# Layered field interactions: a table of matmul kinds for even, odd and last chunks, fewer low parts on VectorE, other ring depths, and sums stored by fours

## The chip, the cores and the metric

The kernel runs on one core of one Trainium2 chip. The metric is the device time in microseconds (us), as a median over runs. Five engines share the work: TensorE (PE, its weight loads are shown as PEld), VectorE (DVE), ScalarE (ACT), GpSimd (POOL) and SyncE (SP), which here only issues transfers.

## The reference

The input `x0` has 512 examples of 39 fields of 16 numbers. Three layers follow each other, each with 128 outputs:

```
xk = x0
for layer in 0, 1, 2:
    z = relu(einsum('bhd,bkd,hks->bsd', x0, xk, W[layer]) + b[layer])
    if layer < 2:
        xk = z[:, :64]           # goes into the next layer
        direct.append(z[:, 64:]) # is only summed
    else:
        direct.append(z)
logit = sum(concatenate(direct, axis=1), axis=-1)   # over the 16 numbers
```

All of it is in 32-bit floating point. Per layer this is a table of products of pairs of fields, contracted with a weight matrix.

## The kernel before

**Tiles.** The 512 x 16 columns are cut into 16 chunks (`CHUNKS`) of 512 columns (32 examples). For each chunk and layer, VectorE multiplies fields into product tiles of 128 rows x 512 columns, and TensorE contracts them into one accumulator `z`. Two tiles make a couple. Layer 0 has 4 couples (780 distinct pairs; the fourth couple is a rest of 12 rows, kept in 76 rows), layers 1 and 2 have 10 each.

**Kinds.** A couple is done in one of three ways, set by a letter in the tables `KINDS`, `KINDS_FIRST` (chunk 0) and `KINDS_SECOND` (layer 0 of chunk 1):
- E (exact): the product stays 32-bit, and TensorE multiplies it in full precision. Nobody else touches it.
- S: ScalarE rounds the product to a high part `hi` (L656), GpSimd subtracts to get the low part `lo` (L515), and TensorE makes three fast passes for each tile: hi by w_hi, hi by w_lo, lo by w_hi.
- D: as S, but VectorE makes the low part itself (`split_lo`, L440) from a product buffer `d_raw` of which there is one.

The last tile of layers 1 and 2 has no hi by w_lo pass, and the rest couple of layer 0 is one pass in all (its low rows are written into the rows above the high ones, 12 x 512, on GpSimd). The tables of before are "SDES", "ESDSESSDSS", "SSDSSESDES" for every chunk but the first.

**Order.** `segments()` gives the order of couples: layer 1 of chunk c; couples `KEPT` to 9 of layer 2 of chunk c-1 (the tail); layer 0 of chunk c+1; couples 0 to `KEPT`-1 of layer 2 of chunk c. VectorE, ScalarE and GpSimd work in about this order, each ahead of TensorE. The work between two layers of a chunk gives the results time: layer 1 of chunk c must be contracted, and its first 64 outputs copied by ScalarE into `maps2` (L675), before VectorE can begin layer 2 of c.

**Lags.** `schedules()` writes out TensorE's order. The lo passes of a couple come `LO_LAGS[layer]` couples behind its hi passes, and at the end of layer 1 all that are pending follow. `D_LAG` is the number of products between a D product on VectorE and its low part.

**Rings.** Buffers are used in rings: E products, S products (`raw`; freed by GpSimd's low part), high parts and low parts (both freed by the lo passes). `spread` holds field pairs, 7 slots of 1 MB.

**ScalarE's order.** `finish_last(c-1)` (layer 2 of the chunk before, into `final`) stands behind the high parts of couples 0 and 1 of layer 2 of c (`FINISH_AT`). TensorE waits for it before it begins layer 2 of c. `COPY_AT` says where the copy of chunk c+1's fields stands in layer 1, `MAPS1_AT` and `MAPS2_AT` where the outputs of layers 0 and 1 are taken over.

**Weights.** The weights of layers 1 and 2 are split once, in chunks 0 and 1, for those tiles that some table has as S or D (`SPLIT_TILES`): ScalarE makes w_hi (L665), GpSimd w_lo (L531), in pieces (`RUNS`).

**Sums.** VectorE reduces `direct` and `final` over the 16 numbers (L447, L453) into `sums`, [128, 2, 512]. SyncE stores two pieces of 480 columns and at the very end two of 32.

Of the kernel before, what the change touches and what calls it, by code (L numbers as in the profile page):

```python
# [6 lines left out]
BATCH = 512  # L7
OUT = 128
HALF = OUT // 2
COLS = 512  # L10
EXAMPLES = COLS // DIM
CHUNKS = BATCH * DIM // COLS
# [5 lines left out]
BLOCK = 32  # L18
ROWS_REST = 2 * BLOCK + REST
TILES = (FIELDS + 1) // 2  # L20
assert (TILES0 - 1) * 128 + REST == PAIRS
LAYER_TILES = (TILES0, TILES, TILES)

# [2 lines left out]


E, S, D = "E", "S", "D"
KINDS = ("SDES", "ESDSESSDSS", "SSDSSESDES")
KINDS_FIRST = ("EEEE", "ESEEEEEEEE", "EESEEESEES")  # L30

EARLY = 2
KINDS_SECOND = E * EARLY + KINDS[0][EARLY:]
COUPLES = tuple(len(k) for k in KINDS)


def kinds(layer, c):

    if (layer, c) == (0, 1):
        return KINDS_SECOND  # L40
    return KINDS_FIRST[layer] if c == 0 else KINDS[layer]


def split_of(layer, c, couples=None):
# [2 lines left out]

def tiles_of(layer, wanted):

    return [t for t in range(LAYER_TILES[layer]) if any(kinds(layer, c)[t // 2] in wanted for c in (0, 1, 2))]  # L50


SPLIT_TILES = [tiles_of(n, S + D) for n in range(3)]
assert SPLIT_TILES[0][:-1] == list(range(len(SPLIT_TILES[0]) - 1)) and SPLIT_TILES[0][-1] == TILES0 - 1
assert KINDS[0][-1] != E and KINDS_FIRST[0] == E * COUPLES[0]
assert all(KINDS[n][-1] != E for n in (1, 2))

LO_LAGS = (2, 1, 1)
D_LAG = 3

EXACT_RING = 4
RAW_RING = 6
HI_RING = 5
LO_RING = 4
QUADS = TILES // 4
SPREAD_RING = 7
W0_CUTS = (0, 2, TILES0)
W0_PARTS = 2

WEIGHT_CUTS = (0, 4, 8, 12, 16, TILES)  # L70
WEIGHTS_AHEAD = 1
WARM = 3

SUM_LAST_AT = 6
SUM_DIRECT_AT = 6
COPY_AT = 2
FINISH_AT = 2
MAPS1_AT = 5
MAPS2_AT = 3

KEPT = 7
LAST = CHUNKS - 1
assert SUM_DIRECT_AT <= SUM_LAST_AT <= KEPT and MAPS1_AT <= KEPT and FINISH_AT <= MAPS1_AT
FIELD_CUTS = (0, 3, 5, 1 + TILES0)

# [122 lines left out]
def cin_kernel(nc, x_fields, x_spread, w0, w1, w2, b, out):  # L210
# [7 lines left out]
    with ctx:  # L218
        def sb(name, shape, dt=fp32):
            return ctx.enter_context(nc.sbuf_tensor(name, shape, dt))  # L220
# [4 lines left out]
        def sem(name):  # L225
            return ctx.enter_context(nc.semaphore(name))
# [13 lines left out]
        lo = sb("lo", [128, LO_RING, 2, COLS], fp32r)  # L240
        direct = sb("direct", [128, 2, COLS])
        final = sb("final", [128, COLS])
        sums = sb("sums", [128, 2, BATCH])

        w0_staged = raw[:, :, :, :].rearrange("p r t c -> p (r t c)")[:, 0:2 * TILES0 * OUT].rearrange(
            "p (t h s) -> p t h s", h=2, s=OUT)
# [29 lines left out]
        z2_evacuated = sem("z2_evacuated")  # L276
        direct_summed = sem("direct_summed")
        last_summed = sem("last_summed")
        stored = sem("stored")

        def wait_multiplied(engine, layer, c, k):

# [30 lines left out]
        def low_part(layer, c, k):  # L313
# [2 lines left out]
                return hi[low_rows(layer, k), PLACE["SD"][layer, c, k] % HI_RING, 0:1, :]  # L316
            return lo[:, USED[layer, c, k] % LO_RING, :, :]

        def z_of(layer, c):
            return z[{(0, 0): 2, (2, LAST): 0}.get((layer, c), layer)]  # L320

# [6 lines left out]
        @block.sync  # L328
        def _(sp):
            def load_fields(c, p):  # L330
                a, e = FIELD_CUTS[p:p + 2]
                if c == 1:

                    if p == 1:
                        return
                    e = 1 if p == 0 else e
                sp.dma_start(fields[:, a:e, :], x_fields[c, :, a:e, :]).then_inc(fields_loaded[p], 16)  # L337

            def load_early(p):
                a, e = FIELD_CUTS[p:p + 2]  # L340
                sp.dma_start(early[:, a:e, :], x_fields[1, :, a:e, :]).then_inc(early_loaded[p], 16)

            def load_spread(c, q):
                slot, count = quad(c, q)
                if count > 1:
                    before, part = divmod(c * QUADS + q - SPREAD_RING, QUADS)
                    wait_multiplied(sp, 2, before, 2 * part + 1)
                elif slot in (3, 4):
                    wait_multiplied(sp, 0, 1, EARLY - 1)
                sp.dma_start(spread[:, slot, :, :], x_spread[c, :, 4 * q:4 * q + 4, :]).then_inc(  # L350
                    spread_loaded[slot], 16)

            def load_weights(n, p):
                a, e = WEIGHT_CUTS[p:p + 2]
                sp.dma_start(w_exact[n][:, a:e, :], (None, w1, w2)[n][:, a:e, :]).then_inc(w_loaded[n][p], 16)

            load_fields(0, 0)
            sp.dma_start(w0_staged[:, W0_CUTS[1]:, :, :], w0[:, W0_CUTS[1]:, :, :]).then_inc(w0_loaded[1], 16)  # L358
            load_fields(0, 1)
            load_fields(0, 2)  # L360
            load_early(0)
            load_early(1)
            for q in range(QUADS):
                load_weights(1, q)
                load_spread(0, q)
            load_fields(1, 0)
            load_fields(1, 2)
            for p in range(QUADS):
                load_weights(2, p)
            for c in range(LAST):  # L370
                for q in range(2):
                    load_spread(c + 1, q)
                if c + 2 < CHUNKS:
                    wait_multiplied(sp, 0, c + 1, COUPLES[0] - 1)
                    for p in range(3):
                        load_fields(c + 2, p)
                for q in range(2, QUADS):
                    load_spread(c + 1, q)

            done = LAST * EXAMPLES  # L380
            sp.wait_ge(direct_summed, LAST)
            sp.dma_start(out[0:OUT, 0:done], sums[:, 0, 0:done]).then_inc(stored, 16)
            sp.wait_ge(last_summed, LAST)
            sp.dma_start(out[OUT:2 * OUT, 0:done], sums[:, 1, 0:done]).then_inc(stored, 16)
            sp.wait_ge(direct_summed, CHUNKS)
            sp.dma_start(out[0:OUT, done:BATCH], sums[:, 0, done:BATCH]).then_inc(stored, 16)
            sp.wait_ge(last_summed, CHUNKS)
            sp.dma_start(out[OUT:2 * OUT, done:BATCH], sums[:, 1, done:BATCH]).then_inc(stored, 16)
            sp.wait_ge(stored, 64)

        @block.vector
        def _(dve):
# [51 lines left out]
            def sum_direct(c):  # L444
                dve.wait_ge(z0_evacuated, 3 * c + 3)
                dve.wait_ge(z1_evacuated, 3 * c + 3)
                nc.vector.tensor_reduce(sums[:, 0, c * EXAMPLES:(c + 1) * EXAMPLES],  # L447
                                        direct[:, c % 2, :].rearrange("p (b d) -> p b d", d=DIM),
                                        AX.X, ALU.add).then_inc(direct_summed, 1)

            def sum_last(c):
                dve.wait_ge(z2_evacuated, c + 1)
                nc.vector.tensor_reduce(sums[:, 1, c * EXAMPLES:(c + 1) * EXAMPLES],  # L453
                                        final[:, :].rearrange("p (b d) -> p b d", d=DIM),
                                        AX.X, ALU.add).then_inc(last_summed, 1)

            def weights_last_split_lo(n):

                last = len(SPLIT_TILES[n]) - 1
                dve.wait_ge(weights_hi[n], len(RUNS[n]))  # L460
                nc.vector.tensor_tensor(w_hi[n][HALF:128, last, :], w_exact[n][HALF:128, TILES - 1, :],
                                        w_hi[n][HALF:128, last, :].bitcast(fp32),
# [313 lines left out]
```

## Time and profile before

| | before |
|---|---|
| median of 3 runs | 562.28 us (562.15 to 562.33) |
| the profiled execution's own time | 562.33 us |
| its span in the profile | 560.5 us |
| PE busy | 551.9 us, 98% |
| DVE busy | 535.9 us, 96% |
| POOL busy | 499.5 us, 89% |
| ACT busy | 379.4 us, 68% |
| granted TensorE clock, mean | 0.999 |

Busy times count each instruction from its start to its end, and instructions of one engine overlap at their edges: a split pass is listed with 0.39 to 0.40 us, but the next one begins about 0.23 us later. So what an instruction costs is read from the distance between starts. The own time stands 1.8 us above the span.

### The profile page before, as it was taken

To read this page: it belongs to the slowest core of one execution; us is meant where nothing else is said; L and a number is where in the kernel's file an instruction comes from. 1 tells how busy PE (TensorE), PEld (TensorE's weight loads), DVE (VectorE), ACT (ScalarE), POOL (GpSimd) and SP (SyncE) were. 2 spreads that over 40 slices of the span, in tenths; PEclk is the share of its full clock that TensorE was granted. 3 is DMA by queue.
4 is the path that set the end of the run, shared out by engine and by line. 5 is a ranking of instruction groups with operands and counts; after the bars stand their busy time and mean duration, and the time that the engine had idled before them with its cause. 6 is when DMAs were issued, how large, how long until landed. Compare 5 with 4: busy or idle time off the path is not lost.

```text
span 560.5 us, 6190 instructions
## 1 busy us (share of the span) xinstructions
PE 551.9 (98%) x2008; PEld 374.9 (67%) x2008; DVE 535.9 (96%) x496; ACT 379.4 (68%) x427; POOL 499.5 (89%) x228
## 2 busy tenths in 40 slices
PE   7999999999999999999999999999999999999997
PEld 2435667667677677777767677677777767677665
DVE  4679999999999999999999999999999999999985
ACT  0436577776858767676776858777676876858662
POOL 0438899899999989999899999989999899999986
PEclk9999999999999999999999999999999999999999
DMA  8997391844828266391845828276391845826200
GB/s 326 418 408 317 132 370 34 325 191 181 344 87 331 108 254 271 146 361 30 331 183 183 342 95 333 98 262 263 150 363 29 333 177 192 333 99 215 81 1 20
DMA packets 21056, 122.17 MB, mean 218 GB/s; under 512 B 2720, under 2 KB 2976, under 8 KB 10784
## 3 DMA queue, kind: packets, MB, share of 16 engines
q1 hardware_dynamic: 20736, 121.51, 56.0%
q8 instruction: 16, 0.26, 0.2%
q10 hardware_dynamic: 288, 0.26, 0.2%
q14 instruction: 16, 0.13, 0.1%
HBM read 121.24 MB, written 0.52 MB: 217 GB/s over the span
## 4 chain that ended last, share of the span: by engine, by line
PE 82%; DVE 10%; issue 3%; ACT 2%; DMA 1%; POOL 1%; SPq 0%; DVEq 0%; POOLq 0%; ACTq 0%
PE z L611 82%; DVE raw L426 4%; DVE exact L426 3%; DVE d_raw L426 2%; DMA fields<-x_fields 1%; DVE lo L440 1%; POOL lo L515 1%; ACT hi L656 1%; ACT maps L675 0%; ACT final L696 0%; ACT L675 0%; DVE sums L453 0%; DVE sums L447 0%; SPq L358 0%; SPq L337 0%
## 5 line engine op out<-in xcount | busy, mean ns | idle before, releaser
L515 POOL TENSOR_TENSOR lo<-raw,hi 128x1024 fp32r<-128x1024 f32 x198 | 469.1, 2410 | 12.1 <-ACT hi L656 11.6
L656 ACT ACTIVATE hi<-raw 128x1024 fp32r<-128x1024 f32 (+1 forms) x213 | 219.1, 1029 | 125.1 <-DVE raw L426 112.0
L611 PE MATMUL z<-hi,w_hi 128*128 128x512 f32 (+1 forms) x559 | 220.8, 399 | 0.9 <-ACT hi L656 0.4
L426 DVE TENSOR_TENSOR raw<-spread,maps 128x1024 f32<-128x1024 f32 x184 | 219.0, 1210 | 2.1 <-ACT maps L675 2.1
L611 PE MATMUL z<-hi,w_lo 128*128 128x512 f32 x513 | 202.5, 395 | 0.0
L611 PE MATMUL z<-lo,w_hi 128*128 128x512 f32 x544 | 196.7, 451 | 0.2 <-POOL lo L515 0.2
L611 PE MATMUL z<-exact,w_exact 128*128 128x512 f32 (+1 forms) x386 | 180.4, 594 | 2.8 <-DVE exact L426 2.0
L611 PEld LDWEIGHTS z<-lo,w_hi 128*128 128x128 f32 x544 | 101.2, 188 | 56.2 <-issue 31.5
L611 PEld LDWEIGHTS z<-hi,w_hi 128*128 128x128 f32 (+1 forms) x559 | 104.8, 188 | 31.4 <-ACT final L696 3.7
L611 PEld LDWEIGHTS z<-exact,w_exact 128*128 128x128 f32 (+1 forms) x386 | 72.1, 189 | 68.0 <-issue 53.7
L611 PEld LDWEIGHTS z<-hi,w_lo 128*128 128x128 f32 x513 | 96.2, 188 | 22.9 <-issue 0.5
L426 DVE TENSOR_TENSOR exact<-spread,maps 128x1024 f32<-128x1024 f32 x76 | 91.4, 1212 | 8.2 <-ACT maps L675 5.7
L656 ACT ACTIVATE hi<-d_raw 128x1024 fp32r<-128x1024 f32 x74 | 75.8, 1025 | 21.5 <-DVE d_raw L426 18.7
L440 DVE TENSOR_TENSOR lo<-d_raw,hi 128x1024 fp32r<-128x1024 f32 x74 | 89.9, 1215 | 0.0
L426 DVE TENSOR_TENSOR d_raw<-spread,maps 128x1024 f32<-128x1024 f32 x60 | 73.3, 1221 | 0.5
L675 ACT ACTIVATE maps<-z,bias 64x512 f32<-64x512 f32 x64 | 41.5, 648 | 3.4 <-PE z L611 2.2
L515 POOL TENSOR_TENSOR hi<-raw,hi 12x512 fp32r<-12x512 f32 x15 | 19.2, 1279 | 18.5 <-ACT hi L656 18.4
L531 POOL TENSOR_TENSOR w_lo<-w_exact,w_hi 128x512 fp32r<-128x512 f32 (+3 forms) x10 | 9.9, 1001 | 22.7 <-ACT w_hi L665 22.7
L426 DVE TENSOR_TENSOR raw<-fields,copies 76x512 f32<-76x512 f32 (+1 forms) x29 | 27.1, 934 | 0.0
L679 ACT ACTIVATE direct<-z,bias 64x512 f32<-64x512 f32 x32 | 21.9, 685 | 0.8
L426 DVE TENSOR_TENSOR exact<-fields,copies 128x1024 f32<-128x1024 f32 x15 | 18.2, 1212 | 0.0
L426 DVE TENSOR_TENSOR d_raw<-fields,copies 128x1024 f32<-128x1024 f32 x14 | 17.1, 1222 | 0.0
(21 smaller groups left out, 69.6 us busy)
## 6 DMA issues: line engine op xcount, KB each, us to landing
spread<-x_spread SPq DMA_DIRECT2D x80, 1024.0 KB, 8.1
fields<-x_fields SPq DMA_DIRECT2D x31, 768.0 KB, 6.8
fields<-x_fields SPq DMA_DIRECT2D x15, 512.0 KB, 5.6
w_exact<-w SPq DMA_DIRECT2D x10, 256.0 KB, 14.7
spread<-x_fields SPq DMA_DIRECT2D x1, 768.0 KB, 10.1
raw<-w SPq DMA_DIRECT2D x1, 640.0 KB, 6.7
spread<-x_fields SPq DMA_DIRECT2D x1, 512.0 KB, 10.7
out<-sums SPq DMA_DIRECT2D x2, 240.0 KB, 4.2
```

What stands on the lines that cost most here:

```text
L426: nc.vector.tensor_tensor(products, by_field, by[0:rows, :].unsqueeze(1).to_broadcast([rows, tiles, COLS]), ALU.mult).then_inc(ready, 1)
L440: nc.vector.tensor_tensor(low_part(layer, c, k), d_raw[low_rows(layer, k), 0:tiles_in(layer, k), :], hi[low_rows(layer, k), place % HI_RIN ...
L515: nc.gpsimd.tensor_tensor(low_part(layer, c, k), raw[low_rows(layer, k), PLACE[S][layer, c, k] % RAW_RING, 0:tiles_in(layer, k), :], hi[lo ...
L531: nc.gpsimd.tensor_tensor(w_lo[n][:, m:m + e - a, :], w_exact[n][:, a:e, :], w_hi[n][:, m:m + e - a, :].bitcast(fp32), ALU.subtract).then_ ...
L611: mm = nc.tensor.matmul(z_of(layer, c)[:, :], w[0:rows, :], part[0:rows, :], start=(step == FIRST_STEP[layer, c] and p == 0), stop=(step = ...
L656: nc.scalar.activation(hi[0:rows, count % HI_RING, 0:tiles, :], products, ACT.Copy).then_inc(hi_ready, 1)
L675: nc.scalar.activation(maps[half * HALF:(half + 1) * HALF, :], z_of(n, c)[0:HALF, :], ACT.Relu, bias=bias[0:HALF, n:n + 1]).then_inc(evacu ...
L679: nc.scalar.activation(direct[n * HALF:(n + 1) * HALF, c % 2, :], z_of(n, c)[HALF:OUT, :], ACT.Relu, bias=bias[HALF:OUT, n:n + 1]).then_in ...
```

## The change

Four things change together.

1. Tables. Even chunks (from 2): "DSES", "SDESSDSSES", "SSDSSESESS". Odd chunks: "DSES", "SDSSESSDES", "SDSSESDESS". Last chunk (15): "SDES", "SDSSSSSDES", "DSESESDSSD". First chunk: "EEEE", "EEEEEEESEE", "EESEESESES". So an even chunk has 4 D instead of 5, an odd one 5, the last 6.
2. Order and depth: `LO_LAGS` (2, 1, 1) to (0, 2, 1); `D_LAG` 3 to 2; rings of E products 4 to 3, S products 6 to 4, high parts 5 to 6, low parts 4 to 5; `KEPT` 7 to 6; `COPY_AT` 2 to 7; `WEIGHTS_AHEAD` 1 to 2.
3. More weight tiles are split, since more couples are S or D in some chunk: 18 tiles of layer 1 (16 before) and 20 of layer 2 (16 before).
4. `sums` is a ring of 8 chunks, and every four chunks are stored at once: SyncE issues two stores of 128 columns (64 KB each) in its loop at c = 5, 9 and 13, and two at the end. VectorE waits for a store before it writes over its place (`wait_stored`).

```diff
+LAST = CHUNKS - 1
-KINDS = ("SDES", "ESDSESSDSS", "SSDSSESDES")
-KINDS_FIRST = ("EEEE", "ESEEEEEEEE", "EESEEESEES")
+KINDS = ("DSES", "SDESSDSSES", "SSDSSESESS")
+
+KINDS_ODD = ("DSES", "SDSSESSDES", "SDSSESDESS")
+KINDS_LAST = ("SDES", "SDSSSSSDES", "DSESESDSSD")
+KINDS_FIRST = ("EEEE", "EEEEEEESEE", "EESEESESES")
...
-KINDS_SECOND = E * EARLY + KINDS[0][EARLY:]
+KINDS_SECOND = E * EARLY + KINDS_ODD[0][EARLY:]
...
-    return KINDS_FIRST[layer] if c == 0 else KINDS[layer]
+    return (KINDS_FIRST if c == 0 else KINDS_LAST if c == LAST else KINDS_ODD if c % 2 else KINDS)[layer]
...
-LO_LAGS = (2, 1, 1)
-D_LAG = 3
-
-EXACT_RING = 4
-RAW_RING = 6
-HI_RING = 5
-LO_RING = 4
+LO_LAGS = (0, 2, 1)
+D_LAG = 2
+
+EXACT_RING = 3
+RAW_RING = 4
+HI_RING = 6
+LO_RING = 5
...
-WEIGHTS_AHEAD = 1
+WEIGHTS_AHEAD = 2
...
-COPY_AT = 2
+COPY_AT = 7
...
-KEPT = 7
-LAST = CHUNKS - 1
+STORED = 4
+
+
+KEPT = 6
...
-        sums = sb("sums", [128, 2, BATCH])
+        sums = sb("sums", [128, 2, 2 * STORED * EXAMPLES])
...
+        def columns(c):
+
+            a = c % (2 * STORED) * EXAMPLES
+            return slice(a, a + EXAMPLES)
+
+        def wait_stored(engine, half, c):
+
+            if c >= 2 * STORED and c % STORED == 0:
+                engine.wait_ge(stored[half], 16 * (c // STORED - 1))
...
+            def store(half, part):
+
+                a = part * STORED * EXAMPLES
+                sp.wait_ge((direct_summed, last_summed)[half], (part + 1) * STORED)
+                sp.dma_start(out[half * OUT:(half + 1) * OUT, a:a + STORED * EXAMPLES],
+                             sums[:, half, columns(part * STORED).start:columns(part * STORED).start
+                                  + STORED * EXAMPLES]).then_inc(stored[half], 16)
...
-            done = LAST * EXAMPLES
-            sp.wait_ge(direct_summed, LAST)
-            sp.dma_start(out[0:OUT, 0:done], sums[:, 0, 0:done]).then_inc(stored, 16)
...
+                if c > STORED and c % STORED == 1:
+                    for half in range(2):
+                        store(half, c // STORED - 1)
+            for half in range(2):
+                store(half, CHUNKS // STORED - 1)
+            for half in range(2):
+                sp.wait_ge(stored[half], 16 * CHUNKS // STORED)
```

## Rows read from the trace of the kernel before

**Rows 1.** The page's head: span, then busy time and instructions of each engine

```profile
span 560.5 us, 6190 instructions
PE 551.9 (98%) x2008; PEld 374.9 (67%) x2008; DVE 535.9 (96%) x496; ACT 379.4 (68%) x427; POOL 499.5 (89%) x228
```

**Rows 2.** Busy time by stretch, the steady part: PE, PEld, DVE, ACT, POOL, clock, DMA

```profile
75.00:500.00 425.00, 424.61 (x1607) 299.95 (x1607) 424.56 (x393) 308.35 (x342) 406.93 (x178) 1.00 0.56 218
```

**Rows 3.** Chain that ended last: start, length, engine, work

```profile
75.62 427.99 PE z L611 x1620
...
545.87 11.40 PE z L611 x41
```

**Rows 4.** Timeline of DVE: start, length, work [idle before it]

```profile
79.35 0.67 DVE L447 TENSOR_REDUCE sums<-direct 128x32 f32<-128x512 f32 x1
...
304.77 0.68 DVE L426 TENSOR_TENSOR raw<-fields,copies 76x512 f32<-76x512 f32 x1
305.37 1.21 DVE L440 TENSOR_TENSOR lo<-d_raw,hi 128x1024 fp32r<-128x1024 f32 x1
306.50 2.34 DVE L426 TENSOR_TENSOR raw<-spread,maps 128x1024 f32<-128x1024 f32 x2
...
515.91 0.67 DVE L447 TENSOR_REDUCE sums<-direct 128x32 f32<-128x512 f32 x1
516.50 0.67 DVE L453 TENSOR_REDUCE sums<-final 128x32 f32<-128x512 f32 x1
...
538.65 2.35 DVE L426 TENSOR_TENSOR raw<-spread,maps 128x1024 f32<-128x1024 f32 x2 [2.11 <-ACT maps L675]
```

**Rows 5.** Timeline of PE, matmuls

```profile
39.89 3.67 PE L611 MATMUL z<-exact,w_exact 128*128 128x512 f32 x8 [0.80 <-issue]
...
298.46 0.63 PE L611 MATMUL z<-lo,w_hi 128*128 128x512 f32 x2
...
299.86 0.63 PE L611 MATMUL z<-lo,w_hi 128*128 128x512 f32 x2
...
302.90 1.88 PE L611 MATMUL z<-exact,w_exact 128*128 128x512 f32 x4
...
305.07 0.40 PE L611 MATMUL z<-hi,w_hi 128*128 128x512 f32 x1
...
540.61 0.96 PE L611 MATMUL z<-hi,w_hi 128*128 128x512 f32 x2
...
545.87 0.73 PE L611 MATMUL z<-lo,w_hi 128*128 128x512 f32 x2 [0.23 <-POOL lo L515]
```

**Rows 6.** Waits between 75 and 500 us: engine, waited for, total, times, longest

```profile
POOL hi L515 <- ACT hi L656: 14.3, 12, 1.2
PEld z L611 <- POOL lo L515: 5.2, 25, 0.2
POOL lo L515 <- ACT hi L656: 3.5, 22, 0.2
PEld z L611 <- ACT final L696: 3.5, 13, 0.8
```

**Rows 7.** Timeline of POOL

```profile
308.88 26.03 POOL L515 TENSOR_TENSOR lo<-raw,hi 128x1024 fp32r<-128x1024 f32 x11
...
341.02 1.28 POOL L515 TENSOR_TENSOR hi<-raw,hi 12x512 fp32r<-12x512 f32 x1 [1.19 <-ACT hi L656]
...
541.04 11.86 POOL L515 TENSOR_TENSOR lo<-raw,hi 128x1024 fp32r<-128x1024 f32 x5 [2.08 <-ACT hi L656]
553.53 2.35 POOL L515 TENSOR_TENSOR lo<-raw,hi 128x1024 fp32r<-128x1024 f32 x1 [0.64 <-ACT hi L656]
```

**Rows 8.** Groups by line: the splitting of the weights, count, busy, mean ns

```profile
L531 POOL TENSOR_TENSOR w_lo<-w_exact,w_hi 128x512 fp32r<-128x512 f32 (+3 forms) x10 | 9.9, 1001 | 22.7 <-ACT w_hi L665 22.7
```

**Rows 9.** Transfers: count, KB each, median us to landing

```profile
out<-sums SPq DMA_DIRECT2D x2, 240.0 KB, 4.2
out<-sums SPq DMA_DIRECT2D x2, 16.0 KB, 1.6
```

More of the change, by code:

```diff
@@ L48, in tiles_of @@
 def tiles_of(layer, wanted):
-    return [t for t in range(LAYER_TILES[layer]) if any(kinds(layer, c)[t // 2] in wanted for c in (0, 1, 2))]
+    return [t for t in range(LAYER_TILES[layer]) if any(kinds(layer, c)[t // 2] in wanted for c in (0, 1, 2, 3, LAST))]
 SPLIT_TILES = [tiles_of(n, S + D) for n in range(3)]
 assert SPLIT_TILES[0][:-1] == list(range(len(SPLIT_TILES[0]) - 1)) and SPLIT_TILES[0][-1] == TILES0 - 1
-assert KINDS[0][-1] != E and KINDS_FIRST[0] == E * COUPLES[0]
-assert all(KINDS[n][-1] != E for n in (1, 2))
-LO_LAGS = (2, 1, 1)
-D_LAG = 3
-EXACT_RING = 4
-RAW_RING = 6
-HI_RING = 5
-LO_RING = 4
+assert all(k[0][-1] != E for k in (KINDS, KINDS_ODD, KINDS_LAST)) and KINDS_FIRST[0] == E * COUPLES[0]
+assert all(k[n][-1] != E for k in (KINDS, KINDS_ODD, KINDS_LAST) for n in (1, 2))
+LO_LAGS = (0, 2, 1)
[4 more added lines that the diff above has]
+LO_RING = 5
 QUADS = TILES // 4
@@ L278, in cin_kernel @@
         last_summed = sem("last_summed")
-        stored = sem("stored")
+        stored = [sem("stored_direct"), sem("stored_last")]
         def wait_multiplied(engine, layer, c, k):
@@ L378, in _ @@
                     load_spread(c + 1, q)
-            done = LAST * EXAMPLES
-            sp.wait_ge(direct_summed, LAST)
-            sp.dma_start(out[0:OUT, 0:done], sums[:, 0, 0:done]).then_inc(stored, 16)
[L383 to L389, printed above, removed]
+                if c > STORED and c % STORED == 1:
[5 more added lines that the diff above has]
+                sp.wait_ge(stored[half], 16 * CHUNKS // STORED)
         @block.vector
@@ L446, in sum_direct @@
                 dve.wait_ge(z1_evacuated, 3 * c + 3)
-                nc.vector.tensor_reduce(sums[:, 0, c * EXAMPLES:(c + 1) * EXAMPLES],
+                wait_stored(dve, 0, c)
+                nc.vector.tensor_reduce(sums[:, 0, columns(c)],
                                         direct[:, c % 2, :].rearrange("p (b d) -> p b d", d=DIM),
@@ L452, in sum_last @@
                 dve.wait_ge(z2_evacuated, c + 1)
-                nc.vector.tensor_reduce(sums[:, 1, c * EXAMPLES:(c + 1) * EXAMPLES],
+                wait_stored(dve, 1, c)
+                nc.vector.tensor_reduce(sums[:, 1, columns(c)],
                                         final[:, :].rearrange("p (b d) -> p b d", d=DIM),
```

## Prediction

> **What bounds the kernel now.** I read the page's head first: PE is busy 98% of the span, DVE 96%, POOL 89% [rows 1]. Between 75 and 500 us both PE and DVE are busy 99.9% of the time and POOL 96%, at full clock [rows 2]. Busy shares can't tell the two apart, since a pass's listed time hides a bubble of up to 0.16 us behind it. So I count starts.
>
> The period of a chunk is the distance of the sums over `direct`: from 79.35 to 515.91 us is 13 chunks, 33.58 us each [rows 4].
>
> PE's own work: two starts that are one split couple apart are 298.46 and 299.86 us, 1.40 us for six passes, 0.2335 us each. From 302.90 to 305.07 us stand one E couple and two lo passes: 2.17 - 0.47 = 1.70 us for the E couple [rows 5]. A chunk has 5 E couples (8.5 us) and, by the tables, 13 + 47 + 47 = 107 fast passes (25.0 us): 33.50 us.
>
> DVE's own work: a full product or low part is 1.13 us (305.37 to 306.50), the rest couple 0.60, a sum 0.59 [rows 4]. A chunk has 23 full products, 5 low parts, the rest, two sums: 31.64 + 0.60 + 1.18 = 33.42 us.
>
> POOL's own work: 26.03 us for 11 low parts in a row, 2.37 each, and 1.28 for the rest [rows 7]. A chunk has 13 and the rest: 32.1 us. The other 1.5 us are waits: 1.19 us before each rest, and twice some 0.16 us, each time for a high part from ACT [rows 6, 7].
>
> So PE would need 33.50 and DVE 33.42 of 33.58 us. Who leads? The waits say it: once per chunk (13 times between 75 and 500 us) the weight load waits 0.2 us for `final` from ACT, and 25 times for a low part from POOL [rows 6]. `final` stands in ACT's order behind the first two high parts of layer 2, and those wait for DVE's products. DVE never waits itself. So DVE sets the pace, its remaining 0.16 us being small gaps, with PE less than 0.1 us behind as the next bound. The chain agrees up to a point: it lists one stretch of PE from 75.62 us for 428 us, and PE again for the last 11.4 us [rows 3].
>
> Where PE does wait: before 75.62 us, while the first chunks load; and at the end. From 540.61 to 545.87 us PE did 17 passes, 3.97 us of work, in 5.26 us: 1.3 us lost [rows 5]. The reason is the last boundary between layers 1 and 2. There is no layer 0 left to fill it, only the three couples of the tail. DVE waited 2.11 us for `maps2`, and POOL 2.08 us after it [rows 4, 7].
>
> **The change part by part.**
>
> *Steady state, DVE.* An even chunk loses one low part: 33.42 - 1.13 = 32.3 us. Odd ones keep 33.4. The mean falls 0.57 us to 32.9. DVE is then well below PE.
>
> *Steady state, PE.* An even and an odd chunk have 5 E couples and 19 split ones with the rest, as before: 33.50 us. So PE becomes the bound, and of DVE's 0.57 us only 33.58 - 33.50 = 0.08 us per chunk can be had. Times 13 chunks: 1.0 us. This is the main limit of the change: at most two tenths of a per cent in the steady part.
>
> *Steady state, POOL.* An even chunk gets one low part more: 14 x 2.37 + 1.28 = 34.5 us, above PE's 33.5; an odd one 32.1. The mean is 33.3, only 0.2 us under PE. So the waits of 1.5 us per chunk must nearly vanish, and POOL must be ahead by enough to cover the uneven stretches. I put PE's and POOL's sums next to each other in the order of the couples. The worst stretch is the tail of an even chunk, S E S S: POOL 7.11 us, PE 5.7. Behind it comes layer 0, where the lag is now 0, so PE asks for the low part of couple 1 right behind its high passes. Counting from the end of layer 1: POOL has done four low parts at 4 x 2.37 = 9.5 us, PE asks after 5.7 + two couples less the low passes of the second = 8.5 us. So POOL needs to be 1.0 us ahead at the end of layer 1 of an odd chunk. Going on by the same sums through the two chunks from a lead of 0 at that place, POOL is 0.05 us ahead at the end of layer 1 of the even chunk (before D E S S, which asks less: 4.74 against 5.7 us), and 1.45 us ahead at the end of layer 1 of the odd one. That is 0.45 more than needed, and the lead grows by about 0.5 us per pair until a ring stops it. The waits of POOL also have less cause: the 1.19 us came since POOL, after one low part of the tail and one of layer 0 (4.74 us), was earlier at the rest than ACT, which must take over layer 1 first. With `KEPT` 6 it has 7.1 to 9.5 us to do there. I cost POOL at nothing in the steady part; if this cover is gone, the price is up to 1.0 us per pair of chunks.
>
> On running POOL and DVE against each other the trace speaks: a low part on POOL took 2.37 us with DVE 99.9% busy, and 2.35 us at 553.53 us, when DVE had only its last reduction left [rows 2, 7]. The Trainium skill, page "SBUF — State Buffer", section "SBUF: two separate sides", says that a DVE operation with two SBUF inputs and a GpSimd operation that reads SBUF lock a shared port pair, and that the other "fully blocks". By that rule the sum of both would bound a chunk, and moving a low part from 1.13 to 2.37 us would cost 1.24 us in each even chunk; the trace disagrees, as 33.4 and 32.1 us of work fit in one period of 33.58.
>
> *Rings, lags, `COPY_AT`.* They add no instruction. S products in flight fall from 6 to 4: DVE may be four ahead of POOL, 9.5 us of POOL's work, so POOL is fed. DVE may block behind that or behind a full ring of low parts, and has 0.6 us per chunk to give. `COPY_AT` 7 puts the copy of the fields in front of seven couples of DVE's work that don't need it. D products are again never closer than the single buffer allows. Nothing, between 0 and the 1.0 us per pair named.
>
> *`KEPT` 6.* It moves one couple of layer 2 behind layer 1. The cover of the boundary from 1 to 2 grows from 4.3 to 5.7 us at the end of the kernel. DVE's first product of the last layer is possible about 1.5 us after layer 1's end, and its high part about 3.9 us after it, so the gap at the boundary is covered. POOL has there three low parts of the tail first, and layer 1 of the last chunk has seven S (16.6 us against PE's 14.1). It needs to be about 1.8 us ahead at the start of that layer beyond its 1.2; the growth over six pairs gives it 3. I take 1.1 of the 1.3 us as saved, bounds 0 and 1.3. On the other side the cover from layer 0 to 1 shrinks from 10.1 to 8.7 us; its chain (ACT 1.3, DVE 1.2, ACT 1.1, POOL 2.4) is 6 us: nothing.
>
> *E couples that become S.* One in layer 2 of chunk 0 and one in layer 1 of chunk 15: 1.70 - 1.40 = 0.3 us each. The first falls before 75.62 us, where PE waits for DVE's chain anyway: nothing. The second counts 0.3.
>
> *The start.* The S of layer 1, chunk 0, goes from couple 1 to couple 7, where its product is long there; PE's waits around couple 1 and the 0.80 us at 39.89 us [rows 5] say that something can be had: 0.5 us, bounds 0 and 0.9. Against it: six more tiles of weights to split, on POOL 9.9 us for 34 tiles in ten pieces [rows 8], so about 0.3 a tile, 1.8 us, in the first 70 us where POOL is tight. One more S in layer 2 adds 2.37 us. By the same sums POOL is then up to 0.5 us late for layer 0 of chunk 2, which lies under the wait that ended at 75.62 us. Nothing, up to 1 us if it does not.
>
> *Sums and stores.* The added waits of DVE (chunks 8 and 12) are for stores issued three chunks before; SP's waits at c = 5, 9, 13 are for sums that are a chunk old, and behind them stand loads for a later chunk. Nothing. The last store grows from 16 to 64 KB: between 1.6 us and 4.2 us for 240 KB [rows 9], nearer the first: plus 0.1.
>
> **Sum.** Steady 1.0, last boundary 1.1, E couple 0.3, start 0.5, less 0.1 for the store: 2.8 us. The profiled execution's own time was 562.33 us, its span 560.5, and the median of the runs 562.28: the profiled one is typical. 562.3 - 2.8 = 559.5 us.
>
> **Rivals.**
> 1. *POOL takes DVE's place (slower).* Place: the low part of couple 1 of layer 0 behind an even chunk's tail, with lag 0. Price: up to 1.0 us per pair, seven pairs. It decides if POOL loses more than 0.2 us per chunk to waits for high parts; before it lost 1.5. Against it: the cause of 1.2 of them goes away, as above. From the point where PE loses 0.4 us per pair the gain of 2.8 us is gone. Half the price gives 559.5 + 3.5 = 563 us, the full one 566.5.
> 2. *Nothing that can be told.* POOL's waits stay in part, and PE waits at the last boundary and at a few evens: steady 0.5, E 0.3, end 0: 561.5 us; span from 561.2 to 562.8.
> 3. *The start eats its share.* The 1.8 us of splitting and the S delay chunk 2 by 1 us: 560.5 to 561.1 us.
> 4. *POOL and DVE exclude each other.* If a low part that moves to POOL held up DVE, each even chunk would pay 1.24 us, seven times 8.7: 571 us. The rows speak against it. It is the page's rule named above.
>
> **Chances.** Forecast (558.7 to 560.4) 0.51; rival 1 0.15; rival 2 0.18; rival 3 0.11; rival 4 0.01; faster than 558.7, if the start gives more, 0.04. A measurement of this kernel can tell 0.2%, 1.1 us, from no change: faster means below 561.2 us, 0.51 + 0.11 + 0.04 = 0.66; rival 2 is no change, 0.18; rivals 1 and 4 are slower, 0.16. The range 558.6 to 562.8 us holds the forecast, rivals 2 and 3.
>
> **What would show it.** Right: a mean distance of the sums over `direct` of 33.50 us in pairs; idle time of DVE of 0.5 us per chunk, waiting for ACT or PE; POOL without the 1.2 us wait before the rest and 99% busy; no gap of PE between 535 and 555 us. Wrong: PE's weight load waits of more than 0.3 us for POOL's low parts, once per pair, in layer 0; a period above 33.6; PE's first pass of layer 2 of chunk 1 later than 75.6 us. What would make the forecast wrong is above all that POOL doesn't get ahead, so that the uneven chunks show in PE.

## The result

The changed kernel takes 559.40 us, median of 5 runs, against 562.19 us before: a ratio of 0.9951, with a 95% interval of 0.9940 to 0.9962. The forecast was 559.5 us.

The head of its page, then the stretch between 75 and 500 us and the waits in it:

```profile
span 558.3 us, 6212 instructions
PE 550.0 (99%) x2012; PEld 378.3 (68%) x2012; DVE 528.2 (95%) x490; ACT 381.6 (68%) x429; POOL 518.9 (93%) x236
```

```profile
75.00:500.00 425.00, 425.00 (x1611) 302.32 (x1610) 421.43 (x390) 309.10 (x343) 422.70 (x185) 1.00 0.59 222
```

```profile
ACT final L717 <- PE z L632: 6.1, 9, 0.8
...
PEld z L632 <- POOL lo L536: 0.7, 3, 0.2
...
POOL lo L536 <- ACT hi L677: 0.6, 1, 0.6
...
PEld z L632 <- ACT final L717: 0.5, 2, 0.2
```

Against [rows 2] DVE is 3 us less busy, POOL 16 us more, and PE has no idle time left. The waits have turned round. Before, PE's weight loads waited 13 times for `final` and 25 times for POOL, and POOL lost 1.2 us before each rest [rows 6]. Now it is ACT that waits for PE to finish a layer before it can write `final`, PE's loads wait for POOL and `final` five times in all, and POOL waited for ACT once. The wait before the rest is gone.

The period is best read from PE itself, at the pass of the rest couple, which is once in each chunk:

```profile
75.17 1.02 PE L632 MATMUL z<-hi,w_hi 76*128 76x512 f32 x2
...
309.90 1.03 PE L632 MATMUL z<-hi,w_hi 76*128 76x512 f32 x2
...
511.10 1.03 PE L632 MATMUL z<-hi,w_hi 76*128 76x512 f32 x2
```

From 75.17 to 511.10 us are 13 chunks, 33.53 us each (33.58 before [rows 4]). This distance from pass to pass is called the period below. The chain that ended last is PE without a break from 73.29 us:

```profile
70.82 2.42 POOL lo L536
73.24 0.04 issue
73.29 481.53 PE z L632 x1825
554.82 0.02 issue
554.84 0.70 ACT final L717
```

This profile is of an execution of 560.07 us, the longest of the five; the others took 559.37 to 559.50, and the difference lies in the first 20 us (last section). Experiment e9 is the changed kernel with other stores at its end only, and its profile has the usual start. So the balance is made with it. Its first pass of layer 2 of chunk 1 is this one:

```profile
75.12 0.39 PE L637 MATMUL z<-hi,w_hi 128*128 128x512 f32 x1
```

Before, it stood at 75.62 us [rows 3], but there the rest pass (0.23 us) was still to come, and in e9 it is done. So the start gave 0.50 + 0.23 = 0.73 us. The 13 chunks took 0.6 us less in e9 (0.65 in the profile above). From the same place in chunk 14 to `final` of the last chunk there are 43.35 us instead of 45.1: 1.75 us. Behind PE's end the changed kernel has 0.2 us more than e9 (558.3 - 554.82 = 3.5 us; e9, with small last stores, has 3.3). That is 0.73 + 0.6 + 1.75 - 0.2 = 2.9 us, against 2.8 measured.

### The profile page after: what moved, and what is told of

Read it like the earlier page. It is cut to its first block, busy times and chain, and to the rows that moved or that the text cites. A ratio compares the mean times of both kernels' runs of the same rounds, so it can differ in the third digit from the quotient of the medians.

```text
span 558.3 us, 6212 instructions
## 1 busy us (share of the span) xinstructions
PE 550.0 (99%) x2012; PEld 378.3 (68%) x2012; DVE 528.2 (95%) x490; ACT 381.6 (68%) x429; POOL 518.9 (93%) x236
## 4 chain that ended last, share of the span: by engine, by line
PE 91%; POOL 3%; issue 2%; DVE 1%; ACT 1%; DMA 1%; ACTq 0%
PE z L632 91%; POOL lo L536 3%; DMA raw<-w 1%; DVE exact L445 1%; ACT maps L696 0%; POOL w_lo L552 0%; ACT L696 0%; DVE raw L445 0%; ACT hi L677 0%; ACT final L717 0%; DVE sums L474 0%; DVE w_exact L497 0%; ACTq L295 0%
## 5 line engine op out<-in xcount | busy, mean ns | idle before, releaser
L536 POOL TENSOR_TENSOR lo<-raw,hi 128x1024 fp32r<-128x1024 f32 x206 | 487.7, 2398 | 9.4 <-ACT hi L677 7.7
L677 ACT ACTIVATE hi<-raw 128x1024 fp32r<-128x1024 f32 (+1 forms) x221 | 225.6, 1030 | 121.6 <-DVE raw L445 112.2
L445 DVE TENSOR_TENSOR raw<-spread,maps 128x1024 f32<-128x1024 f32 x192 | 228.3, 1209 | 3.0 <-POOL lo L536 1.5
L632 PE MATMUL z<-hi,w_hi 128*128 128x512 f32 (+1 forms) x563 | 227.7, 409 | 0.0
L632 PE MATMUL z<-lo,w_hi 128*128 128x512 f32 x548 | 192.0, 440 | 0.2 <-POOL lo L536 0.2
L459 DVE TENSOR_TENSOR lo<-d_raw,hi 128x1024 fp32r<-128x1024 f32 x68 | 82.6, 1215 | 2.6 <-ACT hi L677 2.1
L677 ACT ACTIVATE hi<-d_raw 128x1024 fp32r<-128x1024 f32 x68 | 69.7, 1025 | 13.4 <-PE z L632 7.5
L445 DVE TENSOR_TENSOR d_raw<-spread,maps 128x1024 f32<-128x1024 f32 x54 | 65.8, 1218 | 3.7 <-ACT maps L696 3.6
L552 POOL TENSOR_TENSOR w_lo<-w_exact,w_hi 128x512 fp32r<-128x512 f32 (+2 forms) x10 | 11.6, 1175 | 23.6 <-ACT w_hi L686 23.6
L717 ACT ACTIVATE final<-z,bias 128x512 f32<-128x512 f32 x16 | 11.0, 688 | 10.6 <-PE z L632 10.5
```

The costliest lines, as they stand in the source:

```text
L445: nc.vector.tensor_tensor(products, by_field, by[0:rows, :].unsqueeze(1).to_broadcast([rows, tiles, COLS]), ALU.mult).then_inc(ready, 1)
L459: nc.vector.tensor_tensor(low_part(layer, c, k), d_raw[low_rows(layer, k), 0:tiles_in(layer, k), :], hi[low_rows(layer, k), place % HI_RIN ...
L536: nc.gpsimd.tensor_tensor(low_part(layer, c, k), raw[low_rows(layer, k), PLACE[S][layer, c, k] % RAW_RING, 0:tiles_in(layer, k), :], hi[lo ...
L552: nc.gpsimd.tensor_tensor(w_lo[n][:, m:m + e - a, :], w_exact[n][:, a:e, :], w_hi[n][:, m:m + e - a, :].bitcast(fp32), ALU.subtract).then_ ...
L632: mm = nc.tensor.matmul(z_of(layer, c)[:, :], w[0:rows, :], part[0:rows, :], start=(step == FIRST_STEP[layer, c] and p == 0), stop=(step = ...
L677: nc.scalar.activation(hi[0:rows, count % HI_RING, 0:tiles, :], products, ACT.Copy).then_inc(hi_ready, 1)
```

## The experiments

On the chips of these runs the kernel before took 562.4 us, against 562.2 beside the changed kernel. So the changed kernel should be at about 559.6 us there, an estimate. Medians are of 4 to 11 runs, e5 of 2.

**e1, five D in every chunk.**

```diff
-KINDS = ("DSES", "SDESSDSSES", "SSDSSESESS")
+KINDS = ("DSES", "SDSSESSDES", "SDSSESDESS")
```

> The changed kernel with the odd table in the even chunks too, so that every chunk but the first and last has five D. Theory A (TensorE bounds the changed kernel at 33.53 us per chunk; VectorE with five D has 33.42 us of work and some 0.16 us of small gaps): the period goes back to about 33.58, 12 or 13 chunks times 0.05 us, +0.6 us on 559.4, so 560.0. Theory B (the fewer low parts on VectorE are where the gain comes from): most of the 2.8 us goes, 561.5 to 562.2. Theory C (GpSimd's extra low part in even chunks costs something): faster than 559.4.

Measured: 562.63 us, ratio to before 1.0006 (0.9997 to 1.0014). All of the gain is gone, five times what theory A said. Yet the steady part behaves as A has it. PE's pass of the rest couple, then PE's and POOL's timeline near 505 us:

```profile
74.22 1.03 PE L632 MATMUL z<-hi,w_hi 76*128 76x512 f32 x2
...
275.43 1.03 PE L632 MATMUL z<-hi,w_hi 76*128 76x512 f32 x2
...
476.86 1.07 PE L632 MATMUL z<-hi,w_hi 76*128 76x512 f32 x2
512.32 1.03 PE L632 MATMUL z<-hi,w_hi 76*128 76x512 f32 x2
```

```profile
509.04 0.72 PE L632 MATMUL z<-lo,w_hi 128*128 128x512 f32 x2 [1.59 <-POOL lo L536]
```

```profile
500.85 2.38 POOL L536 TENSOR_TENSOR lo<-raw,hi 128x1024 fp32r<-128x1024 f32 x1 [1.13 <-PE z L632]
504.24 4.75 POOL L536 TENSOR_TENSOR lo<-raw,hi 128x1024 fp32r<-128x1024 f32 x2 [1.01 <-ACT hi L677]
508.94 1.27 POOL L536 TENSOR_TENSOR hi<-raw,hi 12x512 fp32r<-12x512 f32 x1
```

Six chunks take 33.53 us each, the next six 33.57: the little lead is used up by then. But the period that ends at 512.32 us is 35.46, 1.9 us too long, and from there to the last `final` another 1.1 us are lost. The place is layer 0 of the last chunk: its table begins with S, and lag 0 wants the low part at once. POOL came for it 1.6 us late, having waited 1.01 us for a high part. The lead of an engine is how far it is ahead of PE in the same couple. VectorE's was 4.1 us in chunk 14 here and 8.3 us in e9, and POOL's is small with it (table under e11). So in this kernel the low parts taken off VectorE are worth little per chunk (0.3 us in all), and 3 us at the last chunk. That it is lead stored up over the chunks, and not the other table of chunk 14, is what e11 shows (below).

**e2, `KEPT` 7.**

```diff
-KEPT = 6
+KEPT = 7
```

> The changed kernel with KEPT 7 as before, so that the tail of layer 2 has three couples. Theory A (a fourth couple covers the last boundary between layers 1 and 2): TensorE waits again about 1.1 us near 540 us, 560.5 us in all. Theory B (the last chunk's table closed that gap, by beginning with D and having five S in layer 2): 559.4, and no wait of TensorE there. Theory C (the cover from layer 0 to 1 mattered in the steady part): the period falls below 33.53, which TensorE's own work forbids.

Measured: 573.42 us, ratio 1.0196 (1.0182 to 1.0210). None of the theories. The period alternates between 34.3 and 33.9 us, so the end can't be read by itself. DVE and POOL around 285 us:

```profile
284.91 1.22 DVE L445 TENSOR_TENSOR d_raw<-spread,maps 128x1024 f32<-128x1024 f32 x1
287.22 1.23 DVE L459 TENSOR_TENSOR lo<-d_raw,hi 128x1024 fp32r<-128x1024 f32 x1 [1.09 <-ACT hi L677]
```

```profile
290.75 2.41 POOL L536 TENSOR_TENSOR lo<-raw,hi 128x1024 fp32r<-128x1024 f32 x1 [0.91 <-ACT hi L677]
294.14 18.95 POOL L536 TENSOR_TENSOR lo<-raw,hi 128x1024 fp32r<-128x1024 f32 x8 [0.98 <-ACT hi L677]
```

In the odd table couple 6 of layer 2 is D. With `KEPT` 7 it is the last couple before layer 1, and `multiply` makes the low part right behind the product: DVE waits 1.09 us for its high part, and with the 1.13 us of the low part the next S product comes 2.2 us later. POOL runs dry twice, 1.9 us per pair. Its own work in a pair is 27 x 2.36 + 2 x 1.27 = 66.3 us; with the waits 68.2, and the pair takes 34.3 + 33.9 = 68.2 us. This is rival 1's mechanism: PE's pair is 67.06 us, so POOL can lose 0.8 us per pair and no more. It costs more than rival 1 said, 1.1 us per pair, and about 7 us more at the start and the end. Whether a tail of three couples uncovers the last boundary can't be read here; e8 asks it from the other side.

**e3, the odd table in the last chunk.**

```diff
-KINDS_LAST = ("SDES", "SDSSSSSDES", "DSESESDSSD")
+KINDS_LAST = ("DSES", "SDSSESSDES", "SDSSESDESS")
```

> The changed kernel with the odd table in the last chunk: five E instead of four, D in other places. Theory A (one E couple more on TensorE, 0.30 us, the boundary stays covered by the fourth couple of the tail): 559.7 us. Theory B (the last table also closes the gap at the end): 560.5 us or more, with waits of TensorE after 540 us.

Measured: 560.69 us, ratio 0.9972 (0.9956 to 0.9983). The period is unchanged, 33.53 us. From the last rest couple to the last `final` it takes 44.95 us instead of e9's 43.74: 1.2 us, of which 0.3 are the E couple. For the rest PE waits at the last boundary again:

```profile
542.61 0.50 PE L632 MATMUL z<-hi,w_hi 128*128 128x512 f32 x1 [0.33 <-ACT hi L677]
```

This is the first and longest of several gaps, 0.9 us in sum. Theory B holds. So the last table is needed too, beside the fourth couple of the tail (e8).

**e4, the old table of the first chunk.**

```diff
-KINDS_FIRST = ("EEEE", "EEEEEEESEE", "EESEESESES")
+KINDS_FIRST = ("EEEE", "ESEEEEEEEE", "EESEEESEES")
```

> The changed kernel with the old table of the first chunk. Theory A: one E couple more in layer 2 (0.3 us) and the S of layer 1 back at couple 1, where TensorE waited for its high part (0.3 us): 559.4 + 0.3 to 0.6 = 559.7 to 560.0 us. Theory B (TensorE waits for GpSimd until 73.3 us anyway, so the first chunk's table is hidden): 559.4 us, or faster, as GpSimd has one low part less to do.

Measured: 561.19 us, ratio 0.9979 (0.9970 to 0.9988), 1.6 us slower than the changed kernel, more than either theory. Its profile has the same late start as the changed kernel's, so the two can be compared: the rest pass of chunk 1 comes 0.6 us later, the next three periods are 37.10, 33.86 and 33.72 us (36.41, 33.52 and 33.55). Near 66 us PE waits for the low part of weights, where the changed kernel has no wait:

```profile
66.01 0.47 PE L632 MATMUL z<-hi,w_hi 128*128 128x512 f32 x1 [0.70 <-POOL w_lo L552]
```

**e5, four D in every chunk.**

```diff
-KINDS_ODD = ("DSES", "SDSSESSDES", "SDSSESDESS")
+KINDS_ODD = ("DSES", "SDESSDSSES", "SSDSSESESS")
```

> The changed kernel with the even table in the odd chunks too, so that GpSimd has 14 low parts and the rest in each of chunks 1 to 14. Theory A (GpSimd's own work, 14 x 2.37 + 1.28 = 34.46 us, becomes the bound of every chunk): the period goes from 33.53 to 34.46 us, 12 or 13 chunks, +11 to 12 us, less what lead it had: 569 to 571.5 us. Theory B (GpSimd is never the bound, VectorE's relief is what counts): 559 us or less. Theory C (VectorE and GpSimd exclude each other, so that only the swap of 1.13 for 2.37 us counts, 1.24 us in seven chunks): 568 us with VectorE idle while GpSimd works.

Measured: 575.01 us, ratio 1.0222 (1.0204 to 1.0241). Between 75 and 500 us:

```profile
75.00:500.00 425.00, 421.41 (x1572) 293.00 (x1572) 406.78 (x375) 303.57 (x337) 424.23 (x187) 1.00 0.58 221
```

POOL is busy 99.8% of the time, and the period is 34.3 us, which is its own work: 14 x 2.36 + 1.27. Theory A has the bound right. It missed what a missing lead costs at both ends: 12 periods of 0.76 us are 9 us, the rest of the 15.4 is the start and the last chunk, whose period is 35.64. While POOL works without a break, DVE is busy 406.78 of 425 us, and its product of 128x1024 takes 1.21 to 1.22 us as before. So the two don't exclude each other: in turns they would need 831 us. This goes against the Trainium skill, page "SBUF — State Buffer", section "SBUF: two separate sides", by which, of a DVE operation with two SBUF inputs and a GpSimd operation that reads SBUF, the one that comes second "fully blocks".

**e6, lag 2 in layer 0.**

```diff
-LO_LAGS = (0, 2, 1)
+LO_LAGS = (2, 2, 1)
```

> The changed kernel with the lag of layer 0's low passes at 2 again. Theory A (GpSimd is ahead by more than the 1.0 us that lag 0 asks): no change in the steady part, 559.4 within 0.2 us. Theory B (lag 0 makes TensorE wait at even tails or at the start): faster by up to 0.5 us, and the wait near 73 us goes. Theory C (a later end of layer 0 delays the first maps and the rest couple): slower by 0.1 to 0.5 us.

Measured: 560.54 us, ratio 0.9968 (0.9956 to 0.9981). About 0.9 us slower, more than theory C gave and not A's "no change"; the period is the same. PE waits for POOL in the last chunk, at 533.99 and 541.04 us, as in e7.

**e7, the old depth of two rings.**

```diff
-HI_RING = 6
-LO_RING = 5
+HI_RING = 5
+LO_RING = 4
```

> The changed kernel with 5 high and 4 low buffers as before instead of 6 and 5. Theory A (POOL's lead, which covers the even chunks' surplus, is held by these rings; one couple less takes about 1.4 us of it, and 1.0 us is asked once per pair): TensorE waits 0 to 0.5 us per pair, 559.4 to 563 us, I expect 560.5. Theory B (the rings are not used up): 559.4 us.

Measured: 560.72 us, ratio 0.9970 (0.9959 to 0.9981). The size is theory A's, the place is not. The period is 33.53 us, so the even chunks' surplus is covered with these rings too. What is lost, 1.1 us, is lost in the last chunk:

```profile
534.24 0.73 PE L632 MATMUL z<-lo,w_hi 128*128 128x512 f32 x2 [0.47 <-POOL lo L536]
541.28 0.74 PE L632 MATMUL z<-lo,w_hi 128*128 128x512 f32 x2 [0.18 <-POOL lo L536]
```

**e8 and e12, the kernel before with `KEPT` 6, alone and with other rings.**

```diff
-KEPT = 7
+KEPT = 6
 # e12 also:
-RAW_RING = 6
-HI_RING = 5
+RAW_RING = 5
+HI_RING = 6
```

> The kernel before with KEPT 6 and nothing else changed. Theory A (a fourth couple in the tail covers the last boundary between layers 1 and 2): 562.2 - 1.1 = 561.1 us, the period still 33.58. Theory B (the gap is closed by other parts of the change): 562.2 us.

> The kernel before with KEPT 6, and with 6 high buffers instead of 5 (and 5 product buffers instead of 6, for room). KEPT 6 alone gave a period of 33.67 us, with ScalarE waiting 20.6 us for TensorE to free high buffers where it waited 7.7 us before. Theory A (those waits are what KEPT 6 costs in the steady part): the period goes back to 33.58, the last boundary stays covered, and the whole comes to 562.4 - 0.8 = 561.6 us. Theory B (the place of couple 7's D, or VectorE's order, costs it): the period stays 33.67 and the time near 563.8.

Measured: e8 563.78 us, ratio 1.0025 (1.0015 to 1.0035); e12 561.77 us, ratio 0.9988 (0.9979 to 0.9997). In both the last rest couple lies 42.3 us before the last `final`, 0.85 us less than the 43.1 of the kernel before. Before, PE did 19 passes (4.4 us of work) in 5.8 us there, from 540.61 to 546.44 us, and so lost 1.4 us. The fourth couple covers 0.85 of it and about half a microsecond stays (e12: 0.69 us from the start at 543.68 us to the next, instead of 0.23). Theory A of e8 was nearly right there (1.1 us) and wrong on the whole, since the period rose to 33.67 us. The wait behind it, between 100 and 500 us of e8 and of e12:

```profile
ACT hi L656 <- PE z L611: 20.6, 30, 1.2
```

```profile
ACT maps L675 <- PE z L611: 6.7, 12, 0.6
```

ACT waited for free high buffers (7.7 us there in the kernel before); in e12 that wait isn't listed any more. Its period is 33.53 us, below the 33.58 expected, with five D in each chunk and DVE busy all the time:

```profile
78.58 0.39 PE L611 MATMUL z<-hi,w_hi 76*128 76x512 f32 x1
...
514.43 0.39 PE L611 MATMUL z<-hi,w_hi 76*128 76x512 f32 x1
```

So PE's bound can be reached without taking a low part off VectorE. The reason can be read from VectorE at the start of the tail, before and in e12:

```profile
329.18 1.21 DVE L440 TENSOR_TENSOR lo<-d_raw,hi 128x1024 fp32r<-128x1024 f32 x1
330.42 1.23 DVE L426 TENSOR_TENSOR d_raw<-spread,maps 128x1024 f32<-128x1024 f32 x1
```

```profile
327.66 1.21 DVE L440 TENSOR_TENSOR lo<-d_raw,hi 128x1024 fp32r<-128x1024 f32 x1
328.79 1.21 DVE L426 TENSOR_TENSOR raw<-spread,maps 128x1024 f32<-128x1024 f32 x1
```

With `KEPT` 7 the tail begins with couple 7, a D, directly behind the low part of layer 1's D. There is one `d_raw`, so the product must wait for that low part, and it starts 1.24 us behind it instead of 1.13. With `KEPT` 6 the tail begins with an S. These 0.11 us are most of the difference between DVE's sum of work and the period of before. In e1's table the tail begins with D again, its DVE has the same 1.25 us, and its period is 33.57 us.

Both e8 and e12 lose about 1 us at the start, where PE waits for POOL's weights (1.30 us near 66 us). The kernel before has no such wait, so it comes with `KEPT` 6. The changed kernel hasn't it either, but e4 has, with 0.70 us: the new table of the first chunk takes it away.

**e9, small last stores.**

```diff
-            for half in range(2):
-                store(half, CHUNKS // STORED - 1)
-            for half in range(2):
-                sp.wait_ge(stored[half], 16 * CHUNKS // STORED)
+            done, kept = LAST * EXAMPLES, (CHUNKS - STORED) * EXAMPLES
+            first, middle = columns(CHUNKS - STORED).start, columns(LAST).start
+            for summed, a, e, at in ((LAST, kept, done, first), (CHUNKS, done, BATCH, middle)):
+                for half in range(2):
+                    sp.wait_ge((direct_summed, last_summed)[half], summed)
+                    sp.dma_start(out[half * OUT:(half + 1) * OUT, a:e],
+                                 sums[:, half, at:at + e - a]).then_inc(stored[half], 16)
+            for half in range(2):
+                sp.wait_ge(stored[half], 16 * (CHUNKS // STORED + 1))
```

> The changed kernel, with the last four chunks' sums stored in two pieces per half: 96 columns when chunk 14 is summed, and 32 at the very end, as the kernel before did at its end. Nothing else differs, so its profile also shows the changed kernel once more. Theory A (the larger last store costs the 0.2 us by which the stretch from TensorE's end to the span's end grew, 3.27 to 3.49 us): 0.2 us faster than the changed kernel. Theory B (the landing hardly depends on the size): no change that can be told.

Measured: 559.31 us, ratio 0.9947 (0.9934 to 0.9959). The 0.2 us show in the profiles (3.3 against 3.5 us behind PE's end). The ratios, 0.9947 and 0.9951, can't tell them: their intervals overlap.

**e10 and e11, D in place of E in three and in five chunks,** on top of e9. A fourth table `("DSES", "SDESSDSSES", "SSDSSESDSS")` is used where

```diff
+    KINDS_FOURTH if c % 4 == 0     # e10: chunks 4, 8, 12
+    KINDS_FOURTH if 4 <= c <= 12   # e11: even chunks 4 to 12
```

> e9, and in chunks 4, 8 and 12 couple 7 of layer 2 is D instead of E. Theory A (TensorE is the bound of the steady part, VectorE has room): three times 1.70 - 1.40 = 0.30 us, 0.9 us faster than e9. Theory B (the lead that VectorE and GpSimd have built up is needed at the last chunk, and the 1.13 us of each D eats it): gain below 0.5 us, or a loss, with TensorE waiting for low parts after 530 us.

> As e10, but in all even chunks from 4 to 12, five of them. Theory A (TensorE's bound alone counts): 1.5 us faster than e9. Theory B (VectorE's 33.42 us of work and its small gaps are back in each of these chunks, 33.58 us in all, above TensorE's mean of 33.38): its lead is used up and the gain is smaller than e10's.

Measured: e10 559.67 us, ratio 0.9944 (0.9930 to 0.9957); e11 561.35 us, ratio 0.9982 (0.9973 to 0.9991). The chunks with the D take 33.22 us, 0.31 less, as TensorE's sum says: PE is the bound. e10 gets 0.9 us that way and gives 0.7 back between the last rest couple and the last `final` (44.41 against 43.74 us). That leaves 0.2 us, and its two executions with the usual start, 559.01 and 559.09 us, lie that much under e9's 559.17 to 559.31; its median is one of three with the late start (last section). e11 is slower than e9: its last period is 35.05 us, and PE waits for POOL again in layer 0 of the last chunk:

```profile
507.62 0.73 PE L638 MATMUL z<-lo,w_hi 128*128 128x512 f32 x2 [1.25 <-POOL lo L542]
```

Theory B holds for both. With e1 these runs show the stored lead. It is read at the rest couple of chunk 14, from the start of VectorE's product, and of POOL's low part, to PE's pass. In e11:

```profile
471.49 0.67 DVE L451 TENSOR_TENSOR raw<-fields,copies 76x512 f32<-76x512 f32 x1
...
475.85 1.03 PE L638 MATMUL z<-hi,w_hi 76*128 76x512 f32 x2
```

| run | VectorE's lead, chunk 14 | POOL's lead, chunk 14 | period to the last rest pass | from there to the last `final` |
|---|---|---|---|---|
| e9 | 8.3 us | 4.5 us | 33.53 us | 43.74 us |
| e10 | 6.7 us | 3.7 us | 33.54 us | 44.41 us |
| e11 | 4.4 us | 2.0 us | 35.05 us | 45.22 us |
| e1 | 4.1 us | 2.5 us | 35.46 us | 44.87 us |

All four have the same rings, lags and last table, and e9, e10 and e11 the same table in chunk 14 too. So what e11 loses in the last chunk was used up in chunks 4 to 12. In the even chunks of the changed kernel VectorE's lead grows from 4.4 us in chunk 2 to 8.3 in chunk 10 and stays there. No version was clearly faster than the changed kernel.

## Why the prediction was right, point by point

- *What bounds.* Right: PE is at its own work. Its sum was 33.50 us, measured 33.53. That DVE set the pace of before fits as well, but its 0.16 us of "small gaps" were not looked into: 0.11 of them are the one D product that waits for the low part in front of it. e12 hasn't this wait and runs five D per chunk in 33.53 us.
- *Steady part, 1.0 us.* Right in that PE becomes the bound, mis-sized: 0.65 us, 13 times 0.05 instead of 0.08, since PE's sum was 0.03 us per chunk too small. That it takes fewer low parts on VectorE was too strong: e12 gets the same by `KEPT` 6 with one high buffer more and one product buffer less.
- *POOL costs nothing, rival 1 with its threshold.* Right for the tables and orders as they are: no wait for the rest, and a lead that grows. But one sum was wrong, and it came out well by luck. Behind S E S S (5.7 us) and two couples less two low passes (2.8 - 0.47 us) PE asks after 8.0 us and not 8.5, so POOL had to be 1.5 us ahead and not 1.0; by the prediction's own 1.45 us that was just missed. The trace has the wait at this place, once and small, in layer 0 of chunk 4:

```profile
140.35 0.30 PEld L632 LDWEIGHTS z<-lo,w_hi 128*128 128x128 f32 x2 [0.19 <-POOL lo L536]
```

  Then the lead of POOL grew by 0.8 us per pair (67.06 - 66.3) and not 0.5. e2 and e5 show the other side: as soon as POOL loses more than its 0.8 us per pair, or has more work than PE, its time is the period.
- *Rings, lag 0, `KEPT`.* That they cost nothing is right, but they are worth something: the two rings 1.1 us (e7) and lag 0 0.9 us (e6), both in the last chunk. The prediction took `KEPT` 6 for the boundaries only. It did not see that with 7 a D would stand last in its segment and cost 1.1 us per pair (e2), nor that 6 costs 1 us at the start with the old first table (e8, e12).
- *The last boundary, 1.1 us, and the last E, 0.3.* Together 1.75 us measured, so 1.45 for the boundary, a little over the upper bound of 1.3: PE had lost 1.4 us there, 0.1 of it behind 545.87 us. Now it has no wait there:

```profile
540.67 0.65 PE L632 MATMUL z<-lo,w_hi 128*128 128x512 f32 x2
541.15 0.40 PE L632 MATMUL z<-hi,w_hi 128*128 128x512 f32 x1
```

  The prediction gave this to `KEPT` 6 alone, if POOL is about 3 us ahead. `KEPT` 6 by itself covers 0.85 us (e8, e12); without the last table 0.9 us are lost again (e3), and without lag 0 or the deeper rings 0.9 to 1.1 us (e6, e7). That POOL must be ahead is confirmed by e1, e10 and e11; the 3 us themselves were not tested.
- *The start, 0.5 us.* 0.73 us measured, inside the bounds of 0 and 0.9. It contains the E couple of chunk 0 that became an S, which was put at nothing; the two were not taken apart. The predicted lateness of POOL before layer 0 of chunk 2 is there, 0.4 us before 73.29 us, where the low part of couple 1 is waited for:

```profile
73.29 0.73 PE L632 MATMUL z<-lo,w_hi 128*128 128x512 f32 x2 [0.22 <-POOL lo L536]
```

- *The last store, 0.1 us.* 0.2 us by the profiles. The eight stores of 64 KB land after 7.6 us at the median, and no engine waited for those of the loop.

The gain was forecast too high in the steady part and at the store (1.0 and -0.1 against 0.65 and -0.2), and too low at the boundary and the start (1.1 and 0.5 against 1.45 and 0.73). The errors nearly cancel, so a hit within 0.1 us is partly luck. Of rival 4 nothing was seen. Rival 3 didn't come about, and e4, which loses 1.6 us with the old first table, suggests that this table is the reason. How much each edit does at the start was not taken apart: `WEIGHTS_AHEAD` was not tried alone.

## What to carry to other kernels

When the engines of a pipeline are within 2% of each other, as here, the period is the largest sum of work, and it moves by hundredths of a microsecond; what an edit is worth is decided at the ends. An engine with slack stores it up as lead, and the last stage, which has nothing behind it to cover a dependency, spends it: a saving that is worth 0.3 us in the steady part was worth 3 us in the last chunk (e1). The lead has to be built up over many chunks and can be used up in them (e11). So ask of each engine how far ahead it is when the last chunk begins, and give that chunk its own table. And before a cut between segments is moved, look at what becomes the last item in front of it (e2) and the first behind it (e12).

## What was not expected of the hardware

The executions of each kernel of this case fall in two groups, mostly 0.7 us apart. The longer ones have a mean granted clock of 0.996 or 0.997, the others 0.999 or 1.0; one execution of e7 (561.41 us) is the exception. In the profiles the clock between 8 and 12 us tells them apart. PE's first two rows and the stretch from 8 to 12 us, of the changed kernel (560.07 us) and of e9 (559.31 us):

```profile
1.45 4.46 PE L641 MATMUL z<-final 128*128 128x512 f32 x6 [1.45 <-DVE final L500]
7.93 11.79 PE L632 MATMUL z<-exact,w_exact 128*128 128x512 f32 x22 [2.02 <-DVE exact L445]
```

```profile
8.00:10.00 2.00, 2.00 (x3) 0.91 (x4) 1.56 (x2) 0.00 (x0) 0.00 (x0) 0.54 1.05 432
10.00:12.00 2.00, 2.00 (x4) 0.79 (x3) 1.35 (x2) 0.00 (x0) 0.00 (x0) 0.61 1.01 420
```

```profile
1.45 5.00 PE L646 MATMUL z<-final 128*128 128x512 f32 x6 [1.45 <-DVE final L505]
7.99 1.98 PE L637 MATMUL z<-exact,w_exact 128*128 128x512 f32 x4 [1.53 <-DVE exact L450]
```

```profile
8.00:10.00 2.00, 1.97 (x4) 0.66 (x4) 1.56 (x2) 0.00 (x0) 0.00 (x0) 1.00 1.04 434
10.00:12.00 2.00, 1.54 (x4) 0.68 (x4) 1.33 (x2) 0.00 (x0) 0.00 (x0) 1.00 0.99 415
```

The three warming matmuls at the start are the same in both, but they took 4.46 us in the first and 5.00 in e9. Behind them PE sat idle for 2.02 us in the first, before the first weights and products were there, and was then granted 0.54 and 0.61 of full speed, close to the lower level of 1.2 GHz; in e9 it was idle for 1.53 us and stayed at 2.4 GHz. The first outputs of layer 0 were taken over at 17.47 and 16.77 us. The other profiles agree: in e4, e8 and e10 PE was idle for 1.89 to 1.91 us and got 0.51 to 0.63, in the nine others for 0.98 to 1.43 us and stayed at full clock. The warming took 4.46 to 4.65 us where the clock fell, and 5.00 to 5.49 us where it did not. Why it differs is open. A longer warming was not tried.
